# Four chained attention layers on one core: TensorE turns the identity 20 times before its first data, VectorE copies one of two turned context chunks, and the five engines' orders are replaced

## What is computed

```python
# layer 0: x = LN-attention over the context (8 heads of 32), then a state scan, then a bias per batch
x = residual + _mha(_layernorm(x, g1, beta1), _layernorm(ctx, g1, beta1), W_qkv, b_qkv, W_o, b_o)
U = (_layernorm(x, g2, beta2) @ W_in.T + b_in) @ Bmat
s = silu(s @ A.T) + u_t                      # over 1024 steps
x = x + states @ Cmat + mod[:, None, :]
# layer 1: attention with LN on both sides, 16 heads of 64, causal
# layer 2: attention on raw q and k, 16 heads of 16, masked, then a LayerNorm of out + residual
# layer 3: attention with LN, 16 heads of 16, masked; then x + fc2(gelu(fc1(LN(x))))
```

## Time and profile before

| | us |
|---|---|
| median of 3 runs | 1286.78 (1285.27 to 1286.94) |
| the profiled execution, its own time | 1289.58 |
| its span | 1287.9 |
| TensorE busy | 1245.3 (97%) |
| VectorE busy | 928.3 (72%) |
| ScalarE busy | 732.5 (57%) |
| GpSimd busy | 568.4 (44%) |

### The profile page before, as it was taken

The page is one execution under the profiler, slowest core; times in us unless marked ns, Lnnn a source line. Parts: engine busy times, 40 slices in busy tenths (PEclk is TensorE's granted clock), DMA queues, the critical chain, the costliest instruction groups (busy, mean ns, idle before and its releaser), DMA issues.

```text
span 1287.9 us, 24763 instructions
## 1 busy us (share of the span) xinstructions
PE 1245.3 (97%) x9539; PEld 1027.9 (80%) x9539; DVE 928.3 (72%) x1916; ACT 732.5 (57%) x1587; POOL 568.4 (44%) x697
## 2 busy tenths in 40 slices
PE   7899999999999999999999999999999999999998
PEld 6799897777778878878787877788887878888776
DVE  4677773588777777777777557777787678778873
ACT  5477776524665555556655524555555555556464
POOL 4364442015634544464454311554445344545452
PEclk9999999999999999999999999999999999999999
DMA  4433314010000100000000101000000010000000
GB/s 105 96 99 95 85 64 151 2 23 1 19 7 1 42 1 6 5 26 5 1 1 2 49 10 22 15 13 1 22 5 2 1 34 5 2 1 17 2 1 22
DMA packets 48470, 34.21 MB, mean 27 GB/s; under 512 B 22177, under 2 KB 45536, under 8 KB 48352
## 3 DMA queue, kind: packets, MB, share of 16 engines
q1 hardware_dynamic: 48304, 32.59, 9.4%
q10 hardware_dynamic: 48, 0.01, 0.0%
HBM read 23.26 MB, written 8.39 MB: 25 GB/s over the span
## 4 chain that ended last, share of the span: by engine, by line
PE 75%; DVE 12%; ACT 5%; POOL 3%; SPq 3%; issue 2%; DMA 1%; DVEq 0%; ACTq 0%; POOLq 0%
PE ps L914 10%; PE ps L879 8%; PE ps L853 8%; PE ps L977 7%; PE ps L988 7%; PE ps L863 6%; PE ps L937 5%; PE ps L821 5%; PE ps L921 4%; PE ps L804 4%; PE ps L1084 2%; DVE mx L1409 2%; DVE zt L1387 2%; SPq L625 2%; PE ps L910 2%
## 5 line engine op out<-in xcount | busy, mean ns | idle before, releaser
L1639 POOL TENSOR_TENSOR rstd<-mv,halfneg 128x1 f32<-128x1 f32 x192 | 106.1, 554 | 395.5 <-DVE mv L1378 394.7
L853 PE MATMUL ps<-wk,tt 128*128 128x308 f32 x512 | 144.8, 424 | 0.0
L1466 DVE TENSOR_TENSOR xt<-xt,ps 128x256 f32<-128x256 f32 x160 | 66.1, 414 | 99.9 <-PE ps L937 50.5
L977 PEld LDWEIGHTS ps<-tt,fc 128*128 128x128 f32 x1024 | 117.8, 192 | 10.9 <-ACT tt L1183 9.2
L1207 ACT ACTIVATE pr<-pr 128x616 f32<-128x616 f32 x128 | 91.5, 716 | 59.9 <-DVE pr L1415 31.1
L977 PE MATMUL ps<-tt,fc 128*128 128x128 f32 x1024 | 123.7, 278 | 0.0
L1678 POOL TENSOR_TENSOR front<-mx,front 128x616 f32<-128x616 f32 x64 | 79.0, 1234 | 90.2 <-DVE mx L1409 89.8
L853 PEld LDWEIGHTS ps<-wk,tt 128*128 128x128 f32 x512 | 93.1, 190 | 30.1 <-issue 2.4
L1183 ACT ACTIVATE tt<-ps,cols 128x128 f32<-128x128 f32 x192 | 77.3, 456 | 69.7 <-PE ps L804 69.6
L1387 DVE TENSOR_SCALAR zt<-xt,mv,rstd 128x256 f32<-128x256 f32 (+1 forms) x160 | 80.5, 503 | 47.6 <-POOL rstd L1639 47.2
L1678 POOL TENSOR_TENSOR pr<-mx,pr 128x616 f32<-128x616 f32 x64 | 81.5, 1273 | 74.2 <-DVE mx L1409 73.5
(11 more groups left out here) (223 smaller groups left out, 2919.2 us busy)
## 6 DMA issues: line engine op xcount, KB each, us to landing
out_dram<-xt SPq DMA_DIRECT2D x64, 128.0 KB, 2.0
xt<-in_x_dram SPq DMA_DIRECT2D x32, 128.0 KB, 2.2
xt<-out_dram SPq DMA_DIRECT2D x32, 128.0 KB, 2.3
fc<-in_L_xattn_fc_w_dram SPq DMA_DIRECT2D x2, 1024.0 KB, 7.0
wk<-in_L_xattn_wkv_dram SPq DMA_DIRECT2D x4, 512.0 KB, 5.6
front<-in_L_xattn_wkv_dram SPq DMA_DIRECT2D x4, 512.0 KB, 4.5
wo<-in_L_xattn_wo_dram SPq DMA_DIRECT2D x1, 1024.0 KB, 6.0
kb<-in_L_xattn_wq_dram SPq DMA_DIRECT2D x1, 1024.0 KB, 5.2
```

Source lines behind the costliest of these rows:

```text
L853: last = mm(bank(lane, k)[:, SFROM[k]:SFROM[k] + HB * KEYS], t[:, lane, kc, :], wk[:, kc, b, h0:h0 + HB * KEYS], start=kc == 0, stop=kc == ...
L977: last = mm(bank(lane, c // 4)[:, c % 4 * P:(c % 4 + 1) * P], fc1[:, kc, c * P:(c + 1) * P], t[:, lane, kc, :], start=kc == 0, stop=kc == ...
L1639: p.tensor_tensor(rstd[:, n:n + 1], mv[:, n, 1:2], halfneg[:, :], ALU.pow).then_inc(done["rstd"], 1)
```

## The change

Three things change.

1. Behind the wait for the identity TensorE turns the identity 20 times into bank 7, and nothing reads it.
2. The `zT` item of chunk 0 is copied by ScalarE, three times with its three gains; that of chunk 1 by VectorE, in the same way. `k0` waits for both items instead of the semaphore `ctx0_set`, which is gone.
3. All five strings of `TURNS` are new (of which the first line of SyncE's is shown, before and after). No other step is added or left out.

```diff
+IDLE_TURNS = 20
...
 def on_act(it):
-    return it[0] in ("w0", "zT", "rawT", "wprog", "a", "wU", "mean")
+    return it[0] in ("w0", "rawT", "wprog", "a", "wU", "mean") or it == ("zT", 0)
...
 def on_dve(it):
-    return it[0] in ("pack", "k0", "v0", "mod")
+    return it[0] in ("pack", "k0", "v0", "mod") or it == ("zT", 1)
...
     "sync": (
-        "aa2a201aaaaa033aaa1aaaaaaaa00211a3a23001a1223300aaa1221aa033011a323aaa2a00a1122a33a01022133301a023a22133aaa01a1a"
...
+        "010aa3aa21aaaaaa2aaaa3a0a02aa121aaaa3a3aa00aa11a22a33a001aa1a3232100221a3a300aa112233001a21233a23000032321111aaa"
...
             pe.wait_ge(ident_set, 1)
+            for k in range(IDLE_TURNS):
+                turn_in(item_place(1)[:, 0:P], ident[:, :], ident[:, :])
...
                     if i == 0:
-                        pe.wait_ge(ctx0_set, KC)
+                        set_up(pe, ("zT", 0), ("zT", 1))
                         set_up(pe, ("w0", 3))
...
                 elif kind == "zT":
-                    if i == 0:
-                        act.wait_ge(set_dve, dve_no["pack", 0])
-                    ac(ctx0[:, i, :], bk[:, 0:AK], ACT.Identity, bias=col["be0"][:, i:i + 1], scale=col["g0"][:, i:i + 1])\
-                        .then_inc(ctx0_set, 1)
-                    if i == 0:
-                        return
-                    for kc in range(KC):
-                        src = item_place(n - i + kc)[:, 0:AK]
-                        ac(ctxT["1"][:, kc, :], src, ACT.Identity, bias=col["be1"][:, kc:kc + 1], scale=col["g1"][:, kc:kc + 1])
-                        last = ac(ctxT["3"][:, kc, :], src, ACT.Identity, bias=col["bec"][:, kc:kc + 1], scale=col["gc"][:, kc:kc + 1])
-                        if kc == 0:
-                            last.then_inc(set_act, 1)
+                    act.wait_ge(set_dve, dve_no["pack", 0])
+                    for dst, gain, bias in ((ctx0, "g0", "be0"), (ctxT["1"], "g1", "be1"), (ctxT["3"], "gc", "bec")):
+                        last = ac(dst[:, i, :], bk[:, 0:AK], ACT.Identity, bias=col[bias][:, i:i + 1], scale=col[gain][:, i:i + 1])
...
+                elif kind == "zT":
+                    dve.wait_ge(set_dve, dve_no["pack", 0])
+                    for dst, gain, bias in ((ctx0, "g0", "be0"), (ctxT["1"], "g1", "be1"), (ctxT["3"], "gc", "bec")):
+                        last = v.tensor_scalar(dst[:, i, :], bk[:, 0:AK], col[gain][:, i:i + 1], col[bias][:, i:i + 1], ALU.mult, ALU.add)
```

More of the change, by code:

```diff
@@ L241 @@
[L241 to L245, removed]
@@ L279 @@
[L279 to L285 removed]
+        "iiiiiiiii02ii0ii1i2i1i21iii0iiii2i1ii0ii0i1320301302102302132013012001301301310230120322302131303121320120032103"
@@ new lines @@
+        "3201302020213101020320212031023013031131202132111130102303231230120202313203221210322013003202133131020310332033"
+        "213121103120320020302100312312321323231013011212323123332121223233132132323332323333"),
+    "vector": (
+        "i1i2i020i021ii13ii231132ii0ii0iiii001100121002223321100200013322331121130032330020000110333110022211333211221131"
+        "3302002332022001131331012012101022032323321211333300220203110000111323222120102011333323121223200303303311110201"
+        "2221032112033232000333111222000303331101001211021023321330022313321122000220031133131022101200210033223321331312"
+        "10222303331110011221330022233323sssssssssssssssasassasasasassaaasaassaaasssaasasaaasaaasssaasaaa0a0a0aa0aa111310"
+        "0322321321000000101101122101132222222321000031011000133210330001013130020123220011002120103021112000002122222121"
+        "1000100211010111313003003000022233232021311112333331133232220201130011111303321200323013220000302203033031121122"
+        "2221110122013033010013312011130310000223322333333111212032002110021222200221231113100323000000221112312333130232"
+        "3313123322232010111103011132023230030123200003022300033331212212122220031300331113002111112021131302200003321333"
+        "3311120223122000110222322002133111100330000220011322233302111233323322203230300110011111112320013033322000032100"
+        "302323313311102222221022003310011302111113321121223302000203323123333131122221212312211101133332212323233bbbbbb3"
+        "b2233b3bbbbbbbbbbb32bb3332bbbb2bb22bb33bbbb3b0111003012330012221200000100301112112012120000321003233003120100020"
+        "2210010311000130313301210110133110120002033221333331203110021022302112222002212311110300030302020231121133312203"
+        "3323313132302220211030111011123202003332210300300032020333131221120202221213033000112303111113311010002023223133"
+        "3213122103021310120222203222100113113003302002232010022231113313333023112332322010111010311103330202202123030030"
+        "0220030133313222222100210211130310032330111113310121000222033333223123231112102100221020302201231113100303220003"
+        "0101323232121103333231133230222021100111113103233022302230001030023002033313122222212201130133100103301211101313"
+        "1021000203322333333222112311212223231212332131113132322232333232303322222333333333333213"),
@@ new lines @@
+    "gpsimd": (
+        "ii20i1i213i00031202012123130003301a121321320a2330101202123313230100221101322333001120013122233301000121312322033"
+        "10022133123023111002332a0011322000001111132000002222001111310222021101332323102133303320003032122000103131101030"
+        "11211302122201102222231033321312333320000301322300100331011102303211111220221100222321b3332322011130332303000233"
+        "2000013112110300311121222200311122222113332332333322331003120000031310000111003021111022012223110222213133332220"
+        "1333320000012332310000310112013031111022222101102023221233313223133303221030003320200103130111003111123102222101"
+        "20222133323213210333033201002033200003311110120033111120222211122233233321102233332233333"),
```

65 lines of the change are left out of this document (22 added, 43 removed).

## The result

| us | before | after |
|---|---|---|
| median | 1286.4 | 1272.51 |
| executions | 1285.27 to 1286.94 (4) | 1270.86 to 1274.71 (4) |
| the profiled execution, its own time | 1289.58 | 1270.86 |
| its span | 1287.9 | 1269.1 |

The ratio is 0.9894, with an interval of 0.9877 to 0.9912: the change takes 13.9 us. The forecast was 9.8 less, 1277.0. Of the two profiled executions the one of before is 3.2 us over its median and the one of after 1.7 under it, so their spans differ by 18.8 us; 4.9 of those are not the change. One of the executions of before that were taken beside the experiments ran for 2506.34 us, about twice as long as all others, and is left out of every median and interval here.

What follows compares the result with a forecast made beforehand. TensorE was taken as the bound, busy 1245.3 of 1287.9 us, leaving 42.6 idle us and slow-clock stretches to win. Terms -3.0 - 6.4 - 1.7 + 1.3 = -9.8 us from 1286.8 gave 1277.0 us, range 1272 to 1283.

Steps and rivals of the forecast that it cites:

- prediction's own last sign: The prediction is wrong at the whole if the stretch behind 200 us becomes over 3 us longer or shorter.
- Part 1: At the start, 20 identity turns cost 0 and raise TensorE's clock by about 6 us: -1.9 us, bounds 0 and 3.
- Rival (a): At the start, the clock is not raised or is lost before 12 us: 1278.9 us, chance 0.14.
- Part 2: At the start, splitting context copies between ScalarE and VectorE brings a turn to 11.6 us (-0.7) and the first key product forward (-0.4).
- Part 3: At 58 us, SyncE's new order issues a store and load sooner, so VectorE's stop goes: -6.4 us, bounds -4 and -6.8.
- the prices 3.72 and 2.7: At the 58 us stop, TensorE's standing time of 3.72 us and 2.7 us for 6.0 us of low clock behind it.
- the prediction's 45%: Share of the time TensorE's work takes on the low clock that is too much: (1.91 - 1.05) / 1.91.
- Part 4: At 138 us, no row broadcast stands right before a load any more, so TensorE's 1.71 us stop goes: -1.7 us.
- Part 5: Lane 3's third-tile load now queues behind wo1 and wkv3, landing at 65 to 66.5 us; with another near 147, +1.3 together.
- Near 147: Two parts of wkv1 (1024 KB) now stand ahead of a store: +0.3 us.
- Behind 200 us: TensorE's 27.3 idle us there were taken to change by 0, with ±3 in the range, neither order seen as better.
- rival (c): The new orders also take waits from the long second part, a sixth of 27.3 us: 1272.5 us, chance 0.10.

Runs made afterwards that it cites:

- turns_40: The kernel after with 40 turns of the identity in place of 20: 1272.11 us, ratio 0.989.
- no_turns: The kernel after without the 20 turns of the identity: 1272.38 us, ratio 0.9892.
- turns_only: The kernel before with the 20 turns of the identity and nothing else: 1286.23 us, ratio 0.9996.
- copies_act: The kernel after with all six copies of the turned context on ScalarE: 1273.47 us, ratio 0.9893.
- stop58_only: The kernel before with two SyncE steps moved at 58 us, a store behind the value transfers and a load behind one mask: 1281.95 us, ratio 0.9957.
- late_order: The kernel before up to the end of phase one, then the order of the kernel after on every engine: 1280.87 us, ratio 0.9954.
- The third move: In the kernel before with three SyncE steps moved (1281.72 us), the one putting a lane 2 load ahead of three row broadcasts at 138 us.
- fill_pauses: The kernel after with 4, 4 and 11 further turns of the identity in the start's pauses: 1270.17 us, ratio 0.9867.
- fill_only: The kernel after with 4, 4 and 11 turns in the start's pauses but without the first 20 turns: 1272.17 us, ratio 0.988.
- early_order: The kernel after up to the end of phase one, then the order of the kernel before on every engine: 1278.54 us, ratio 0.9939.
- fill_moved: fill_pauses with lane 3's store and load issued ahead of the weights wo1 and wkv3: 1269.93 us, ratio 0.9868.

## Why the prediction was right, and where it was wrong

The direction was right, and the time lies in the range, but only just (1272.51, and the range begins at 1272); 9.8 us were forecast and 13.9 measured. That it lies there at all is partly luck: two terms brought nothing, and a gain of 6 us came from a place for which the sum had 0. By the prediction's own last sign, a stretch behind 200 us that is over 3 us shorter, it is wrong at the whole; the fixed piece is 6.7 us shorter.

- **Part 1, the clock (-1.9): this step failed.** "If 20 turns raise the clock by about 6 us and it stays up": it rose (between 7.7 and 8.3 us in after, at some 4.3 in turns_40), and did not stay. The turns cost 0 as worked out, and in the median they bring 0 (no_turns, turns_only); in after's own profile, where the clock fell late, 0.9 us against that of no_turns. Rival (a) named it: lost before 12 us. My reason against it was that no pause is over 1.7 us; the runs show the clock falling in a stretch where TensorE has work for 1.76 of 4 us, none of whose pauses is longer than 1.4.
- **Part 2, the copies (-1.1).** The turn came at 11.62 (forecast 11.6), and the value transfers 2.6 us earlier, of the 3.0 forecast for parts 1 and 2. What the copies are worth in time stayed open: copies_act is 1.0 us slower than after by the medians and level by the ratios.
- **Part 3, the stop at 58 us (-6.4): mechanism right, its prices not.** SyncE's two steps alone give 5.0 (stop58_only; the interval, 3.9 to 7.1, has room for 6.4). But the prices 3.72 and 2.7 were those of one odd execution; late_order, with the same order there, shows 1.45 us and 3.4 us of low clock where it had 3.72 and 6.8. At the prediction's 45% that makes 3.0 us and not 6.4, so by the median some 2 of the 5.0 came in another way, and no run shows which.
- **Part 4, the stop at 138 us (-1.7): failed.** The third move adds nothing that can be measured (4.7 with it, 5.0 without). The price 1.71 was again that of the odd execution: in the four other profiles with before's order here VectorE waits 2.6 to 3.0 us and TensorE 0.2 to 0.6.
- **Part 5, the new wait (+1.3): mechanism right, price 0 here.** The load landed at 66.3 (forecast 65 to 66.5), and VectorE waited 1.41 us; TensorE did not. In some profiles it is longer, 2.57 to 2.61 us with TensorE idle for 0.92 to 0.97 between 50 and 150: in fill_pauses and fill_only, and in copies_act, whose start is the slowest of all with this order (first mix at 33.65), so a faster start is not its cause. Moving the step takes it away without a change of the time that can be measured. Near 147, where the sum had +0.3, after's VectorE has no wait for a load.
- **Behind 200 us (0): this term failed most.** The late order alone is worth 5.9 to 6.1 us. This was rival (c), with a chance of 0.10; its number, 1272.5, is the one measured, though by 7.9 and 6.0 us and not by its 9.8 and 4.5. I had read TensorE's waits for their largest group, the norms, and stopped there; the gain is in four smaller ones (7.1 us down to 1.4), at turns and scores that stood too close behind VectorE's and ScalarE's softmax steps. That the moves of these steps made these waits go is read from the groups; the runs isolate the late orders of the five engines together, and that of one engine alone was not run.

The early parts sum to 9.8 forecast and 7.9 measured, the late one to 0 and 6.0. SyncE's two steps gave 5.0 by themselves, in the old order. If they give the same within the new one, the other 2.9 belong to the copies and to the rest of the early order together, and no run divides them.

## What to carry to other kernels

In a hand-ordered kernel the queue of the DMA issues is a list to tune like any other: two moved lines, a store ahead of unrelated loads and a load ahead of three masks, gave 5 us by themselves, of 13.9 for the whole change. An earlier start is worth only what the waits behind it let through (2.4 us sooner gave nothing in the old order; in the new one a start with the clock kept up went with 2.3 less at the end). And before calling a long stretch even, group its waits and add up all the groups: many waits of 0.3 to 1 us are what reordering takes away, and before one profile's longest stop is priced, its time and its mean granted clock should be held against those of the other executions: here the profile of before was like only three of 40 others, and its two stops cost TensorE 3.72 and 1.71 us where the same order cost 1.45 to 2.14 and 0.2 to 0.6 in other profiles.

## What was not expected of the hardware

**The clock of the start stayed up only with both the early turns and the filled pauses.** With 20 turns ahead of the first data alone it fell at 11.0 us (after), 9.9 (turns_only), 9.8 (early_order) and 9.0 (copies_act), and with 40 at 11.2. With the fills alone it was low until some 11.5 and then stayed up, too late to help. With both it stayed up, and the executions of fill_pauses and fill_moved also lie closer together than after's (1269.19 to 1271.0, and 1269.71 to 1270.79, against 1270.86 to 1274.71).

**When the same turns raise it differs from execution to execution.** In after the six weights' turns behind the 20 took 1.84 us, and the clock was up only for the pair at 8.33; in turns_40 it was up at some 4.3 us, with the same instructions up to there. In fill_moved, again with the same instructions so far,

```profile
1.59 3.95 PE L727 MATMUL ps<-ident 128*128 128x128 f32 x20 [1.59 <-POOL ident L1573]
```

the turns took 3.95 us instead of 4.53, and four weights' turns 0.66. The Trainium skill, "TensorE: Matmul & The Clock Gate" (Part 1), says that the number of slow matmuls at a kernel's start varies between runs with the phase at which it begins. These rows agree that it varies; on what it depends no run here shows. One profile of a start therefore says little of the median.
